# A two-block language-model tower: padding rows written early, new issue orders, and products in parts of the array side by side

## What is computed

```
h = table[x]                                                   # 16 x 128 indices
h = h + LN(linear_attention(LN(h)))                            # elu+1 features, 16 heads, causal
h = h + (LN(h) @ CB.T) * (SCB/127) + bias                      # dequantised layer
v = LN(h);  h = h + LN(x + relu(x W1) W2), x = LN(v + performer(v))   # 16 heads, 64 random features
h = h + moe(LN(h)) + shared(LN(h))                             # 8 experts, top 1, 256 -> 512 -> 256
```

## Time and profile before

| | us |
|---|---|
| median of 3 runs (lowest, highest) | 783.99 (782.88, 784.55) |
| the profiled execution: its time | 782.66 |
| its span (first to last instruction) | 780.8 |
| TensorE busy | 691.7 |
| VectorE busy | 478.2 |
| ScalarE busy | 275.1 |
| GpSimd busy | 224.5 |

### The profile page before, as it was taken

The page is one execution under the profiler, slowest core; times in us unless marked ns, Lnnn a source line. Parts: engine busy times, 40 slices in busy tenths (PEclk is TensorE's granted clock), DMA queues, the critical chain, the costliest instruction groups (busy, mean ns, idle before and its releaser), DMA issues.

```text
span 780.8 us, 15276 instructions
## 1 busy us (share of the span) xinstructions
PE 691.7 (89%) x5738; PEld 562.8 (72%) x5739; DVE 478.2 (61%) x1186; ACT 275.1 (35%) x664; POOL 224.5 (29%) x387
## 2 busy tenths in 40 slices
PE   3768999999999999999999999999986089999995
PEld 3547878888888878888888878889885045665653
DVE  2459777777687778777787777776756113222231
ACT  1115544353444344353444344354431012222221
POOL 3543313233241314233141323233222301212111
PEclk9969999999999999999999999999999579999998
DMA  7950000000000000000000000000026711111110
GB/s 269 378 210 1 2 2 1 15 1 15 1 16 1 15 2 15 15 1 15 1 16 1 16 1 15 16 1 16 15 95 223 155 54 54 61 51 60 60 61 16
DMA packets 14911, 38.29 MB, mean 49 GB/s; under 512 B 3195, under 2 KB 9472, under 8 KB 13440
## 3 DMA queue, kind: packets, MB, share of 16 engines
q1 hardware_dynamic: 11056, 26.91, 10.0%
q0 software_dynamic: 3792, 10.51, 4.4%
HBM read 28.74 MB, written 9.58 MB: 49 GB/s over the span
## 4 chain that ended last, share of the span: by engine, by line
PE 83%; issue 6%; DVE 3%; ACT 3%; DMA 2%; POOL 2%; POOLq 0%; DVEq 0%; SPq 0%; ACTq 0%
PE ps L1031 75%; PE ps L1036 5%; PE ps L1196 2%; DMA sorted_rows<-pads,pad_slots 1%; POOL sorted_rows L461 1%; ACT qkA L634 1%; DVE S_sb L724 1%; ACT yTB L624 1%; PE ps L1325 0%; DMA H<-table,idx_sb 0%; DVE stats L658 0%; DMA yA<-sorted_rows 0%; ACT kf L548 0%; PE ps L1169 0%; PE ps L1105 0%
## 5 line engine op out<-in xcount | busy, mean ns | idle before, releaser
L383 POOL TENSOR_TENSOR var_eps<-mv,ln_eps 128x1 f32<-128x1 f32 x112 | 24.1, 215 | 383.5 <-DVE mv L659 383.5
L1031 PE MATMUL ps<-yTC,we 128*128 128x128 f32 x1024 | 127.1, 278 | 0.5 <-ACT yTC L577 0.5
L1031 PEld LDWEIGHTS ps<-yTC,we 128*128 128x128 f32 x1024 | 119.1, 192 | 5.7 <-issue 5.0
L1031 PE MATMUL ps<-we,yTA 128*128 128x256 f32 (+1 forms) x288 | 97.3, 477 | 3.5 <-DVE yTA L754 1.9
L1031 PEld LDWEIGHTS ps<-we,yTA 128*128 128x128 f32 x288 | 55.6, 199 | 29.1 <-issue 21.2
L1031 PE MATMUL ps<-we,yTB 128*128 128x256 f32 (+1 forms) x216 | 72.4, 466 | 0.0
L384 POOL TENSOR_TENSOR rstd<-var_eps,pow_half 128x1 f32<-128x1 f32 x112 | 69.3, 619 | 8.8
L1031 PE MATMUL ps<-we,ffT 128*128 128x256 f32 x256 | 62.0, 386 | 0.0
L1031 PEld LDWEIGHTS ps<-we,yTB 128*128 128x128 f32 x216 | 38.6, 190 | 23.2 <-issue 21.0
L1031 PEld LDWEIGHTS ps<-we,ffT 128*128 128x128 f32 x256 | 46.3, 190 | 5.0
L470 POOL DMA_INDIRECT out<-tmpA,home x12 | 11.8, 985 | 132.1 <-DVE tmpA L1020 132.1
(11 more groups left out here) (199 smaller groups left out, 1366.9 us busy)
## 6 DMA issues: line engine op xcount, KB each, us to landing
we<-w_experts SPq DMA_DIRECT2D x8, 1536.0 KB
home<-sorted_rows SPq DMA_DIRECT2D x23, 128.5 KB, 2.1
we<-w_ff SPq DMA_DIRECT2D x2, 1024.0 KB
rows_sb<-rows SPq DMA_DIRECT2D x1, 1664.0 KB, 7.0
yA<-sorted_rows SPq DMA_DIRECT2D x12, 128.0 KB, 2.1
yB<-sorted_rows SPq DMA_DIRECT2D x11, 128.0 KB, 2.1
we<-w_qk SPq DMA_DIRECT2D x2, 512.0 KB, 4.2
we<-w_v SPq DMA_DIRECT2D x2, 256.0 KB, 4.4
```

What stands on the lines that cost most here:

```text
L383: link(pool.tensor_tensor(var_eps[:, k:k + 1], mv[:, k, 1:2], ln_eps[:], ALU.add))
L1031: return pe.matmul(o, a, b, start=start, stop=stop)
```

## The change

1. The 8 indirect padding writes, `pad_slots` and `pads_known` are gone. Instead SyncE writes padding into all 16 x 8 x 128 rows of the regions at the start, one DMA for the n-th tile of all 8 regions, between the spare tile and the expert loads. `scat(t)` waits until the rows it can reach are written; part two waits for the last group.
2. A new table of PSUM banks, and with it new `after` waits. Those on `scores_masked` now name the number of masks that is needed (`* 4 + 1`, `* 4 + 2`); `b_qT` has none.
3. New orders on TensorE, VectorE, ScalarE and GpSimd. On TensorE `b_kmB, b_q, a_s` now stand next to each other, and so do `b_k, b_h, a_num, b_dg, a_den`.

```diff
-        dgT, T0, qk0, v0, nd0, denT0 = (ps[:, 7, :], ps[:, 6, :], ps[:, 0, :], ps[:, 6, :], ps[:, 2, :], ps[:, 4, :])
+        dgT, T0, qk0, v0, nd0, denT0 = (ps[:, 2, :], ps[:, 4, :], ps[:, 2, :], ps[:, 1, :], ps[:, 4, :], ps[:, 2, :])
...
-        sc = [ps[:, 2, :], ps[:, 4, :], ps[:, 3, :], ps[:, 5, :]]
-        xk = ps[:, 3:5, :]
-        xq = ps[:, 4:6, :]
-        qT = ps[:, 5:7, :]
+        sc = [ps[:, 0, :], ps[:, 5, :], ps[:, 2, :], ps[:, 6, :]]
+        xk = ps[:, 6:8, :]
+        xq = ps[:, 3:5, :]
+        qT = ps[:, 6:8, :]
...
+        def cleared_with(n):
+            return 0 if n < 4 else 1 if n < 10 else 2
...
-            sp.dma_start(sorted_dram[E * SPAN * P:, :], pads[:]).then_inc(S["pad_tile_stored"], 16)
+            sp.dma_start(sorted_dram[E * SPAN * P:, :], pads[:]).then_inc(rows_cleared[0], 16)
+            regions = sorted_dram[0:E * SPAN * P, :].rearrange("(e n p) r -> n p e r", e=E, p=P)
+            for n in range(T):
+                sp.dma_start(regions[n], pads[:].unsqueeze(1).broadcast_to([P, E, ROW])
+                             ).then_inc(rows_cleared[cleared_with(n)], 16)
...
-            sp.wait_ge(S["pad_tile_stored"], 16)
-            sp.wait_ge(S["pads_stored"], 16 * E)
+            sp.wait_ge(rows_cleared[2], 16 * (T - 10))
...
             def scat(t):
+                pool.wait_ge(rows_cleared[cleared_with(t)], 16 * (5, 6, T - 10)[cleared_with(t)])
...
-            pool.wait_ge(S["pads_known"], 1)
-            for e in range(E):
-                pool.indirect_dma_start(out=sorted_dram, in_=pads[:], in_offset=None,
...
-            then(dve.tensor_tensor(pad_slots[:], base[:], partition.broadcast_to([P, E]), ALU.add))
-            dve.sem_inc(S["pads_known"], 1)
...
 b_qT
-                after(pe, "scores_masked", (min(t + 3, T - 1)) * 4 + 4)
-                after(pe, "src0T_ready", min(t + 4, T - 1) + 1)
+                after(pe, "out0_read", min(t + 2, T - 1) + 1)
+                after(pe, "counts_read", t - 1)
...
 TensorE
-                (4, b_kmB), (3, a_ffn), (1, a_v), (5, c_T5), (4, b_q), (5, c_fa), (2, a_rdenT), (5, c_fb),
-                (4, b_ctx0), (5, c_f1), (4, b_ctx1), (5, c_f2), (2, a_out), (4, b_ctx2), (3, b_T3), (4, b_ctx3),
-                (1, a_s), (0, a_T0), (3, b_qk), (4, b_qT), (0, a_qk), (6, c_up), (4, b_h), (3, b_k), (4, b_denT),
-                (6, c_cn), (1, a_num), (3, b_dg), (4, b_rdenT), (1, a_den), (6, c_dn), (2, a_T2), (3, b_kmT),
-                (4, b_out), (3, b_dgT), (5, c_T6), (3, b_v), (5, c_lo), (5, c_ga), (1, a_denT),
+                (6, c_lo), (4, b_kmT), (5, b_out), (1, a_v), (6, c_ga), (2, a_rdenT), (6, c_up), (5, c_T5),
+                (4, b_kmB), (4, b_q), (1, a_s), (5, c_fa), (5, c_fb), (2, a_out), (5, c_f1), (3, b_T3), (0, a_T0),
+                (6, c_cn), (4, b_ctx0), (5, c_f2), (4, b_ctx1), (3, b_qk), (4, b_ctx2), (4, b_qT), (4, b_ctx3),
+                (6, c_dn), (0, a_qk), (3, b_k), (4, b_h), (1, a_num), (3, b_dg), (1, a_den), (2, a_T2), (5, c_T6),
+                (4, b_denT), (3, b_v), (1, a_denT), (4, b_rdenT), (2, a_ffn), (3, b_dgT),
...
 VectorE, new
+                (6, c_norm), (0, a_stats), (1, a_x), (3, a_norm2), (1, a_max), (1, a_elu), (0, a_norm), (5, b_rec),
+                (4, b_km), (4, b_vo), (5, b_mean), (2, a_rec), (3, a_ff), (6, c_log), (5, b_o), (4, kmx),
+                (6, c_choose), (1, a_vz), (5, b_x1), (4, b_dgr), (2, a_mean), (6, c_gc), (6, c_hid), (3, b_norm),
+                (4, b_ks), (4, b_qs), (4, b_keps), (1, a_m2), (1, a_m3), (2, a_o), (1, a_m0), (6, c_slot), (5, c_o),
+                (1, a_m1), (2, a_res), (4, b_cx), (5, c_res), (6, c_down),
 ScalarE, new
+                (4, b_dgc), (2, a_rd), (3, a_yT2), (6, c_yT2), (5, b_wide), (1, a_par), (5, b_rrd), (2, a_wide),
+                (2, a_rrd), (6, c_th), (5, c_yT), (4, b_ek), (5, c_ra), (5, c_rb), (4, b_eq), (3, b_yT), (0, a_yT),
+                (3, b_x), (6, c_tt), (6, c_send), (3, b_sq), (4, b_rqT), (4, b_cx2), (3, b_rk), (0, a_exp), (4, b_rd),
```

More of the change, by code:

```diff
@@ L176, in bass_lm_tower @@
         slot_u = sb("slot_u", [P, 1], U32)
-        pad_slots = sb("pad_slots", [P, E], U32)
         rt = sb("rt", [P, 6 * E])
@@ L207, in bass_lm_tower @@
         gathered = [sem(f"gathered{t}") for t in range(GATHERED_ALONE)]
+        rows_cleared = [sem(f"rows_cleared{n}") for n in range(3)]
         x_loaded = [sem(f"x_loaded{s}") for s in range(MOE_SLOTS)]
@@ L1060, in a_qk @@
                 pe.wait_ge(S["src0T_ready"], t + 1)
-                after(pe, "ctx_even", t - 3)
+                after(pe, "ff2_read", t - 4)
+                after(pe, "scores_masked", (t - 1) * 4 + 1)
                 by_channel(qk0, yTA, qk0_sb, range(4)).then_inc(S["qk0_psum"], 1)
@@ L1073, in a_s @@
                 pe.wait_ge(S["qz_ready"], t * 2 + 2)
-                after(pe, "qexp_in", t - 2)
-                after(pe, "ff2_read", t - 3)
+                after(pe, "src5T_ready", t - 3)
+                after(pe, "hT_ready", t - 4)
                 for half in range(2):
@@ L1086, in a_num @@
                 pe.wait_ge(S["scores_masked"], t * 4 + 4)
+                after(pe, "tile_done", t - 4)
                 for half in range(2):
@@ L1109, in a_rdenT @@
                 pe.wait_ge(S["rden0_wide"], t + 1)
-                after(pe, "kexp_in", t - 1)
+                after(pe, "logit_copied", t - 3)
                 transposed(rdenT0, rdenTA).then_inc(S["rden0T_psum"], 1)
@@ L1114, in a_out @@
                 pe.wait_ge(S["src1T_ready"], t + 1)
+                after(pe, "ffa_ready", (t - 3) * 4 + 4)
                 by_token(o0[:, 0:D], yTA1, out0_sb, KD).then_inc(S["out0_psum"], 1)
@@ L1129, in b_T3 @@
                 pe.wait_ge(S["src3_ready"], t + 1)
+                after(pe, "qexp_in", t)
                 transposed(T3, yB).then_inc(S["src3T_psum"], 1)
@@ L1139, in b_v @@
                 pe.wait_ge(S["src3T_ready"], t + 1)
+                after(pe, "xk_read", t + 1)
                 by_token(v1[:, 0:D], yTB, v1w_sb, KD).then_inc(S["v1_psum"], 1)
@@ L1153, in b_dg @@
                 pe.wait_ge(S["square_ready"], t + 1)
-                after(pe, "rden1_ready", t)
+                after(pe, "x_ready", min(t + 3, T - 1) + 1)
                 for c in range(4):
@@ L1161, in b_dgT @@
                 pe.wait_ge(S["diagT_out"], t + 1)
-                after(pe, "tile_done", t - 2)
                 pe.transpose(dg[:, 0:P], dgT_sb[:], id_sb[:]).then_inc(S["diag_psum"], 1)
@@ L1167, in b_kmT @@
                 pe.wait_ge(S["kmax_ready"], t + 1)
-                after(pe, "diagT_out", t + 1)
+                after(pe, "rden1T_out", t)
                 pe.transpose(km[0:HEADS, 0:P], kmax[:, 0, :], id_sb[:]).then_inc(S["kmaxT_psum"], 1)
@@ L1175, in b_kmB @@
                 pe.wait_ge(S["kmax_head"], t + 1)
+                after(pe, "v0_ready", min(t + 3, T - 1) + 1)
                 matmul(kb[:, 0:HEADS], one16[:], km_diag[:], True, True).then_inc(S["kmax_psum"], 1)
@@ L1182, in b_k @@
                 pe.wait_ge(S["qk1_ready"], t * 4 + 4)
-                after(pe, "scores_masked", (min(t + 2, T - 1)) * 4 + 4)
+                after(pe, "qT_ready", t)
+                after(pe, "out0_read", min(t + 1, T - 1) + 1)
                 features(xk, KD).then_inc(S["xk_psum"], 1)
@@ L1187, in b_q @@
                 pe.wait_ge(S["qk1_ready"], t * 4 + 4)
-                after(pe, "rden0_ready", min(t + 2, T - 1) + 1)
+                after(pe, "src1T_ready", min(t + 2, T - 1) + 1)
                 features(xq, 0).then_inc(S["xq_psum"], 1)
@@ L1209, in b_ctx0 @@
                 pe.wait_ge(S["v1_ready"], t + 1)
-                after(pe, "gC_ready", t - 1)
+                after(pe, "ffb_ready", (t - 1) * 4 + 4)
                 contexts(t, 0)
@@ L1236, in b_denT @@
                 pe.wait_ge(S["den1_out"], t + 1)
-                after(pe, "hT_ready", t - 1)
                 transposed(denT1, denB).then_inc(S["den1T_psum"], 1)
@@ L1256, in c_fa @@
                 pe.wait_ge(S["src5T_ready"], t + 1)
+                after(pe, "gC_ready", t)
                 by_channel(fa, yTC, ff1_sb, range(4)).then_inc(S["ffa_psum"], 1)
@@ L1260, in c_fb @@
                 pe.wait_ge(S["src5T_ready"], t + 1)
-                after(pe, "ffn0_read", min(t + 2, T - 1) + 1)
+                after(pe, "kexp_in", min(t + 1, T - 1) + 1)
                 by_channel(fb, yTC, ff1_sb, range(4, 8)).then_inc(S["ffb_psum"], 1)
@@ L1271, in c_f1 @@
                 pe.wait_ge(S["ffa_ready"], t * 4 + 4)
+                after(pe, "scores_masked", (min(t + 4, T - 1)) * 4 + 1)
+                after(pe, "hT_ready", t)
                 second_layer(t, 0)
@@ L1293, in c_up @@
                 pe.wait_ge(S["src6T_ready"], t + 1)
-                after(pe, "out0_read", min(t + 4, T - 1) + 1)
-                after(pe, "logit_copied", t + 1)
                 by_channel(up, yTC2, su_sb, range(KE)).then_inc(S["up_psum"], 1)
@@ L1302, in c_cn @@
                 pe.wait_ge(S["onehot_ready"], t + 1)
```

(2 more changed lines are left out.)

27 lines of the change are left out of this document (9 added, 18 removed).

## The result

| | before | after |
|---|---|---|
| median, us (lowest, highest; runs) | 784.10 (782.88, 784.55; 4) | 753.02 (749.15, 757.02; 4) |
| the profiled execution: time, span | 782.66, 780.8 | 749.15, 747.3 |
| TensorE busy | 691.7 | 679.7 |
| restart of TensorE for part two | 625.65 | 593.97 |
| written to HBM, MB | 9.58 | 41.10 |

The ratio is 0.9606 [0.9549, 0.9664]: 31 us less, where 39 had been forecast. The spread of the changed kernel, 8 us, is as large as that miss. A ratio leaves out executions more than 1.5% above the fastest of their kernel.

What follows compares the result with a forecast made beforehand. TensorE was taken to set the pace, idle 1.6 us per 35.00 us unit. 780.8 - 20.5 - 10.9 + 4 + 2 - 13 = 742.4 span, + 1.9 and + 1.3 for the median: about 745 us, range 732 to 765.

Steps and rivals of the forecast that it cites:

- exact waits: TensorE before `b_qT`: the wait for masks it doesn't need goes, 13 times, -20.5 us in all.
- products side by side: TensorE's narrow products: 6 fewer changes of shape per unit at 0.13 us each, over 14 tiles' worth of units, -10.9 us.
- new stalls: TensorE in the new orders: near misses charged at 0.3 us per unit, 13 units, +4 us.
- late start: Start of the front part: `a_norm2` of tile 0 behind the statistics step delays its second block 0 to 5 us, +2.
- hand-over: Between front part and part two: indirect padding writes gone, TensorE restarts at 612.6 instead of 625.65, -13 us (-11 to -14).
- traffic of the padding beside the front part: 33.6 MB written from about 27 to 115 us at 376 to 412 GB/s, with `scat` not waiting and TensorE undisturbed.
- 8 borders: Alternative count of only borders between narrow blocks and whole-array products: 8 fewer per unit, saving 14.6 us instead of 10.9.
- Times 14 tiles: Multiplier of the 0.78 us per unit saved on changes of shape: some 14 tiles' worth of units with TensorE the bound.
- The tight `b_rdenT`: Tightest near miss in TensorE's new list: 1.23 us needed after `b_denT`, with only `b_v` and `a_denT` between.
- the rival built on them: A new stall takes the old one's place, TensorE again standing 1.6 us per unit: 762 us, 20 in 100.
- The lower bound, 98: Slowest price for padding writes, 98 GB/s from the indirect ones: 343 us, done by 370, `scat` still not waiting.
- the padding starves TensorE: Rival: with DMA engines full TensorE issues far fewer matmuls; slower than before, at worst 816 us, 4 in 100.

Runs made afterwards that it cites:

- e4: The kernel before with one number changed: `b_qT` waits for the first mask of the tile instead of all four; 0.972, -22.0 us.
- e1: The new orders, banks and waits, with the padding written as before (8 indirect writes after the last tile); 0.9736, -20.7 us.
- e5: e4 with the early padding paced as in e3, all orders and banks old; 0.9529, -36.9 us.
- e3: The changed kernel with one padding write per unit, each waiting on SyncE until TensorE is through `a_den` of the previous tile; 0.9501, -39.1 us.
- e6: e3 with two whole-array steps, `a_T2` and `c_T6`, moved between the narrow products of their block; 0.9737.
- e9: e3 with `a_norm2` ahead of `a_stats` in VectorE's list, as before the change; 0.9574.
- e2: The old orders, banks and waits of the kernel before, with the early padding; 0.9929, -5.6 us.
- e7: The changed kernel, padding unpaced and written from 64 partitions with two rows each, packets of 4104 bytes in place of 2052; 0.9706.
- e8: As e3, but each padding write waits for `a_qk` instead of `a_den`, so that it runs beside the narrow products; 0.9605.
- e11: The changed kernel, unpaced, with the first padding write waiting until the gathers have landed; 0.9528, from two of six runs.
- e12: The changed kernel with its rows 2304 bytes apart in place of 2052, the padding writing the same bytes; 0.9608.
- e10: e3 with the first padding write also waiting until the gathers have landed; 0.9552.

## Why the prediction came out as it did

The time, 753.0, lies in the range and 8 us above the forecast. Term by term, with the ratios above turned into us of 784:

| term | forecast | measured | by |
|---|---|---|---|
| exact waits | -20.5 | -22.0 | e4 |
| products side by side, new stalls, late start | -10.9 + 4 + 2 = -4.9 | +1.3, not told from 0 | e1 less e4 |
| hand-over | -13 | -15 to -18 | e5 less e4, e3 less e1 |
| traffic of the padding beside the front part | 0 | +8 | after less e3 |

**Exact waits.** Right, and mis-sized by 0.19 us per unit, nearly all of it the overlap of two products that a gap doesn't count (e4).

**Price of a change of shape.** 0.13 us was near: 0.165 by e6. Six fewer should give 0.8 to 1.0 per unit; 33.22 - 32.55 = 0.67 came out, 0.11 each, if all of it is theirs. The rule that counts each change of mode held in the rows above, and 8 borders (1.0 per unit) would have been further off.

**Times 14 tiles.** This is the term that was mis-sized in the second row. The saving is paid only where a unit holds all steps. In filling and emptying the new lists lose: `b_h` of tile 2 starts at 145.22 in e1 and at 139.18 in e4, 6.0 us earlier. At 0.67 per unit that is just made up by `b_h` of tile 11, at 438.14 in both. As the pipeline empties e1 gets ahead, by 5.8 us at `c_lo` of tile 14, and loses it again in the last tile: `c_lo` of tile 15 starts at 571.39 and 572.34, VectorE's last front step at 580.19 and 579.52. I had walked the lists through a steady unit and charged the ends 2 us. Which steps lose was not found (e9 was to tell).

**New stalls, 0.3 per unit.** None: 0.02 us. The tight `b_rdenT` and VectorE's 83% cost a steady unit nothing, and the rival built on them has no row for it.

**Padding.** The writes were priced at 376 to 412 GB/s, the rate of reads the earlier trace rows. The engines write these rows at 170, so it takes twice as long. The lower bound, 98 (108, counted from the first of those indirect writes at 603.80), had been kept, but only to ask whether `scat` would wait. The DMA engines are then full to about 240 us and not 115, and with pacing 8 us come back (e3). In the traces the changed kernel loses 3.0 us against e3 between `a_s` of tile 3 and of tile 4, around the gap of 2.01 us, and 3.2 in the three units that are longer than 32.55. That is the rival "the padding starves TensorE" in small: its gaps are there, 2.01, 0.81 and 1.71 us in the changed kernel, one of them between 50 and 120 us as the text had named for the wrong case. Even with the rate right, no row of the trace of before would have sized this term: the only hint was the earlier trace rows, read as all or nothing.

**Hand-over.** Right in each step: the table, 1.74 us (2 forecast), the load, the restart 13.7 us nearer to VectorE's last step. Wrong in one: part two starts faster than before, and is 1.9 us shorter in these traces. In the traces from `c_lo` of tile 15 to the end, e3 needs 174.8 us and e1 188.1, 13.4 less; the 2 to 5 us that the medians show beyond it lie within the spread of e3's runs, 738.7 to 747.0.

**The signs named beforehand.** Right: the waits at `b_qT`, the steady unit (32.55 in 32.5 to 33.3), 0.89 and 0.99 us in the block, the load after the table. Wrong: DMA full to 130 us with TensorE undisturbed; it was full to about 240.

**What the unnamed gaps are.** Counting TensorE's records in the traces, those of its sequencer included, shows where they stand. From 50 us to the hand-over, and beside the waits at `b_qT`, there are ten unnamed gaps of 0.5 us or more: three in the changed kernel, one in e2, two in e7, one in e8, three in e11. They end behind 1217, 2497, 3777 and, in e8, 8641 records, in the old order (e2) as in the new: at the same place each time, plus a multiple of 256. In the changed kernel:

```profile
86.07 0.41 PE L1030 MATMUL ps<-S_sb,den_oneA 128*32 128x128 f32 x4 [2.01 <-issue]
...
152.27 0.27 PE L1105 MATMUL ps<-id_sb,denA 128*128 128x128 f32 x1 [0.81 <-issue]
...
217.23 0.86 PE L1030 MATMUL ps<-S_sb,den_oneA 128*32 128x128 f32 x24 [1.71 <-issue]
```

e11 has its three at these very products, and e7 its two at the first two. In every one of the ten a packet of the instruction queue (q8) landed 1.4 to 3.9 us before TensorE went on. So the gaps stand between two blocks of instructions, whatever products are there. (The Trainium skill, "Runtime: NRT & Kernel Launch", Instruction fetch mechanics, has blocks fetched over a DMA queue, one ahead, mostly hidden; by these gaps not always.)

**What stays open.** Why a block comes late isn't shown. The gaps appear only where the DMA queue has a backlog, and e1, e3, e4 and e5 have none from 60 us on. But e12 has none either, with 16 writes queued and its engines full until about 130, so neither load nor backlog is enough by itself.

ScalarE's pause of 14 to 17 us near 25 us stands in the traces of e6, e7, e9, e10, e11 and e12, in e8 as 11.7 us near 29, and not in those of e1 to e5 and the changed kernel. Neither the padding (e10) nor its rate (e12) is the cause, and each kernel was seen in one trace only. The chip may be: the new orders had no pause on the chip of e1 and e3, and had one in all seven traces on the other two; e5, with the old orders, had none on one of these. So what e6 to e12 lose against e3 or the changed kernel is in part this pause, and none of those differences is the price of the edit alone.

The version to take is e3: 743.95 us, 0.9501, from one added wait, though it ran on one chip only. e5 (0.9529), which keeps the old orders, isn't told from it, and its runs spread over 2 us in place of 8. e12's row pitch and that wait were not tried together.

## What to carry to other kernels

Look for the wait that asks for more than it needs before touching an order: one number gave 22 of the 31 us, all new orders together nothing that can be told from zero, with or without the padding beside them. Work moved off the end into a busy stretch isn't free because its queue is idle: pace it at one piece per unit, and price writes by writes of the same row, not by reads. Walk a new order through the filling and the emptying too, not only through a steady unit. And where an engine stands in the middle of a step with no releaser, count its instructions from one such gap to the next.

## What was new about the hardware

- Writes of 2052-byte rows that lie 2052 bytes apart move about 170 GB/s; the same rows 2304 bytes apart 374. Two rows in one packet (4104 bytes) give 191.
- Under a full DMA load single gaps of 0.7 to 4.3 us appear on TensorE, most in the middle of a step, with no releaser and a multiple of 256 records apart; and an indirect write of one tile took over 21 us to land.
- A change of shape costs about 0.12 us, between two narrow products of different shape too (0.89 to 1.01 us for `b_h`).
- Blocks of instructions are packets of a queue of their own. That queue in the changed kernel in the unit of 34.46 us, engines full, and in the 33 us from 261 on, engines quiet:

```profile
q8 instruction: 3, 0.05, 0.6%
...
q8 instruction: 2, 0.03, 0.4%
```

0.6% of 16 engines for 34.46 us is 3.3 us for three, 0.4% for 33 us is 2.1 us for two: 1.1 us each, in both. If instructions come late under load, it isn't in these stretches their transfer that is slow; the delay would lie in front of it or behind it.
